# 16-head attentions: values and divisors from one product, divided on VectorE

## The chip, the cores and the metric

The kernel runs on one core of a Trainium2 chip. The metric is the device time of one execution in microseconds; the median of three runs is given with the lowest and the highest. Engines are TensorE (PE, its weight loads PEld), VectorE (DVE), ScalarE (ACT), GpSimd (POOL) and SyncE (SP), which issues most DMAs.

## What is computed

32 sequences of 128 rows and 128 columns go through four layers. Each layer adds to x an attention over a context of 128 rows and 96 columns, and then a feed-forward stage or, in one case, a self-attention with a mixture of experts. All is fp32. Three of the attentions have 16 heads of 8 columns, and they are what the change touches:

```python
x = x + _L0_xattn_ref(_layernorm(x), ctx_768, ...)           # cross: biases, output projection
...
x = x + _L2_xattn_ref(_layernorm(x), ctx_768, mask, ...)     # masked: no projection
x = x + _L2_ffn_ref(_layernorm(x), ...)                      # begins with a causal self-attention, gated
# in each of the three, per head of 8 columns:
attn = softmax(q @ k.T * scale)      # 128 x 128
out = attn @ v                       # 128 x 8
```

The other stages (a one-head and an 8-head attention, experts of four kinds) are not changed but for names.

## The kernel before, in words

The kernel is one program with a phase for each stage. `attention16` builds three of them: cross (`a0_`), masked (`a2_`) and self (`b2_`, `causal`). A phase works on 32 items, one sequence each. It is software-pipelined: `unrolled(last)` yields ticks (called steps here), and in each step every engine runs its stages in an order written out by hand, each stage for another item (`item(lag)`). Each engine takes its instructions in order; between engines there are only semaphores.

The stages of a step that matter here:
- TensorE, cross and masked (L542 on): `pe_turn` (L418, queries and keys turned), `pe_stack_k` and `pe_stack_q` (L424), routing products, `pe_values(e, it, 0)`, turns of the normalised rows, `pe_scoresT` for the first half (L472), `pe_scores` for the first half (L457), `pe_values(e, it, 1)`, the projections (L409, L410), the output product (L514), and the second halves of scores. `pe_stack_q` waits for the maxima of both halves. The self stage has its own order (L519 on).
- `pe_values` (L477 to L493) multiplies the exponentials `P` (keys by queries, one block a head) from the left: with `what == 0` by the item's values in `vx`, with `what == 1` by `ones_x`. In both, four heads of a group are accumulated into the same 32 rows of the bank `OB`; four groups make 128 rows. So `OB[:, 0:128]` holds the values turned (head column by query) and `OB[:, 128:256]` the sums of each head, repeated on its 8 rows. An fp32 product is two instructions in the profile: 32 for the values and 32 for the ones, an item.
- VectorE: `v_max` (L711) takes the row maxima of half an item's scores out of PSUM; `v_heads` (L715 to L724) takes the reciprocal of 128 columns of sums (L719) and multiplies (L723) into `oT`, which the output product reads. In the cross and masked stages the order is keys (L703), statistics, casts, norm, `v_max` first half, `aggregate`, `v_heads`, routing, `v_qkv` (L597 or L600, L610 or L613), residual, `v_max` second half. In the self stage it is `v_max` first half, norm, `v_qk_norm` (L652 on), `v_heads`, routing, `v_max` second half, `v_rotate` (L628 to L641).
- GpSimd in the self stage raises 20 columns to the power -1/2 (L821) between `v_rotate` of one step and `v_qk_norm` of the next.
- `vx` is zero but for the values: head j of a group has its 8 columns at 8j in a block of 32.

Of the kernel before, what the change touches and what calls it, by code (L numbers as in the profile page):

```python
# [18 lines left out]
ALU = mybir.AluOpType  # L19
# [53 lines left out]
def build(nc, a, out):  # L73
    ctx = ExitStack()
    with ctx:
# [134 lines left out]
        ones_x = sb("ones_x", [T, 4, 4, DH])  # L210
# [6 lines left out]
        rec = sb("rec", [D, T])  # L217
# [25 lines left out]
        N_CONSTS = 14  # L243
# [60 lines left out]
        def attention16(p, before, kind, post=None):  # L304
# [26 lines left out]
            s_av, s_rec, s_o = sem("av"), sem("rec"), sem("o")  # L331
            s_out, s_xb, s_done = sem("out"), sem("xb"), sem("done")
# [49 lines left out]
            def pe_post_route(e, item):  # L382
                post["pe_read_by_v"](e)
                if item(O + post["LOGITS"]) or post["last_of"](item(O + post["PLACE"])):
                    e.wait_ge(s_o, at(s_o, issued["av"]))
# [91 lines left out]
            def pe_values(e, it, what):  # L477


                if what == 0:  # L480
                    issued["av"] += 1
                    e.wait_ge(s_exp, at(s_exp, 2 * it.n + 2))
                    e.wait_ge(s_v, at(s_v, it.n + 1))
                    if due(it.n):
                        e.wait_ge(s_o, at(s_o, it.n))
                for j in range(4):
                    for g in range(4):
                        lhs = vx[:, it.s, 128 * j + 32 * g:128 * j + 32 * g + 32] if what == 0 else \
                            ones_x[:, j, :, :].rearrange("p a d -> p (a d)")
                        m = e.matmul(OB[32 * g:32 * g + 32, what * T:(what + 1) * T], lhs,  # L490
                                     P[:, it.s % 2, 4 * g + j, :], start=(j == 0), stop=(j == 3))
                if what == 1:
# [26 lines left out]
            def tensor(e):  # L519
# [6 lines left out]
                if causal:  # L526
                    for item in unrolled(last):
# [6 lines left out]
                        if it := item(L + 3):  # L534
                            pe_values(e, it, 0)
                        if it := item(L + 1):
# [4 lines left out]
                        if it := item(L + 3):  # L541
                            pe_values(e, it, 1)  # L542
# [14 lines left out]
                else:  # L557
                    for item in unrolled(last):
# [7 lines left out]
                        if it := item(L + 3):  # L566
                            pe_values(e, it, 0)
                        if post:
# [7 lines left out]
                        if it := item(L + 3):  # L576
                            pe_values(e, it, 1)
# [137 lines left out]
            def v_heads(e, it):  # L715
                if due(it.n):
                    e.wait_ge(s_o, at(s_o, it.n))
                e.wait_ge(s_av, at(s_av, it.n + 1))
                e.reciprocal(rec[:, :], OB[:, T:2 * T]).then_inc(s_rec, 1)  # L719
                if due(it.n - RING + 1):  # L720
                    e.wait_ge(s_out, at(s_out, it.n - RING + 1))
                e.wait_ge(s_rec, at(s_rec, it.n + 1))
                e.tensor_tensor(oT[:, it.s, :], OB[:, 0:T], rec[:, :], ALU.mult).then_inc(s_o, 1)  # L723
# [2032 lines left out]
```

## Time and profile before

| | before |
|---|---|
| median of 3 runs | 1946.26 us (1944.96 to 1949.05) |
| the profiled execution | 1934.08 us |
| its span, first to last instruction | 1932.3 us |
| PE busy | 1597.6 us, 83% |
| DVE busy | 1342.6 us, 69% |
| ACT busy | 959.0 us, 50% |
| POOL busy | 824.1 us, 43% |
| products with values (L490, `vx`) | 116.5 us |
| products with ones (L490, `ones_x`) | 103.7 us |
| reciprocals of the sums (L719) | 89.8 us |
| granted TensorE clock, mean | 0.916 |

The cross stage fills the span from about 45 to 300 us, the masked one from about 785 to 1060, the self one from about 1070 to 1412. Busy time counts an engine's instructions and not its waits. The granted clock is a share of 2.4 GHz; it has two levels, 1.2 and 2.4 GHz, and a figure between is a mean over a stretch with both.

### The profile page before, as it was taken

How to read it: one execution, taken by the hardware profiler on the slowest of the kernel's cores; microseconds unless marked ns; L12 is line 12 of the kernel's file. 1: busy time of each engine (PE TensorE's matmuls, PEld its weight loads, DVE VectorE, ACT ScalarE, POOL GpSimd, SP SyncE). 2: the span in 40 equal slices, each digit the busy share in tenths (PEclk: the TensorE clock that was granted, in tenths of full speed). 3: DMA queues.
4: the chain of work that ended last, by engine and by line, in shares of the span. 5: the costliest groups of instructions: out<-in, count | busy, mean ns of one | idle time of the engine just before them, and what ended most of it. 6: DMA issues, size and time to landing. Idle time of an engine off the chain costs nothing. (4 is left out here: it accounts for less than half of the span.)

```text
span 1932.3 us, 43308 instructions
## 1 busy us (share of the span) xinstructions
PE 1597.6 (83%) x14686; PEld 1248.9 (65%) x14686; DVE 1342.6 (69%) x4056; ACT 959.0 (50%) x1953; POOL 824.1 (43%) x1300
## 2 busy tenths in 40 slices
PE   5999985977799989788997699999849699999840
PEld 3666664966577778565664466666639598888730
DVE  4878873348787777677775688888647488888522
ACT  2666662533333334366665477777725344444310
POOL 2334444346300000111111777799654555565426
PEclk9989997987799999699999699999969899999965
DMA  6657304821000000000000000000029100000043
GB/s 193 226 181 233 102 12 133 250 71 41 17 1 2 1 1 1 6 8 8 8 7 2 1 2 2 2 9 9 9 80 262 45 15 13 19 20 19 11 147 87
DMA packets 60807, 108.72 MB, mean 56 GB/s; under 512 B 11715, under 2 KB 49620, under 8 KB 59796
## 3 DMA queue, kind: packets, MB, share of 16 engines
q1 hardware_dynamic: 54452, 93.45, 15.6%
q0 software_dynamic: 6144, 12.60, 2.2%
q8 instruction: 116, 1.90, 0.4%
q14 instruction: 95, 0.78, 0.1%
HBM read 89.49 MB, written 52.17 MB: 73 GB/s over the span
## 5 line engine op out<-in xcount | busy, mean ns | idle before, releaser
L711 DVE TENSOR_REDUCE parts<-PS 128x8 fp32r<-128x1024 f32 x192 | 234.5, 1221 | 145.2 <-PE PS L457 145.0
L928 ACT ACTIVATE P<-PS 128x1024 f32<-128x1024 f32 x192 | 198.1, 1032 | 105.4 <-PE PS L472 105.2
L905 ACT CAST qS<-PS 32x512 fp32r<-32x512 f32 x384 | 220.8, 575 | 9.5 <-PE PS L424 6.1
L274 POOL TENSOR_TENSOR ve<-mv,eps_t 128x1 f32<-128x1 f32 x160 | 31.7, 198 | 403.9 <-DVE mv L270 403.5
L1757 DVE SCALAR_TENSOR_TENSOR X<-PS,wt,X 128x128 f32 (+1 forms) x480 | 134.9, 343 | 46.1 <-PE PS L1600 38.3
L1889 ACT ACTIVATE P<-PS,w_f_b 128x512 f32<-128x512 f32 x128 | 88.0, 687 | 142.4 <-PE PS L1581 140.9
L1600 PEld LDWEIGHTS PS<-w_f_w,P 128*128 128x128 f32 x1024 | 129.9, 193 | 39.7 <-issue 27.7
L1600 PE MATMUL PS<-w_f_w,P 128*128 128x128 f32 x1024 | 141.8, 282 | 13.6 <-DVE X L1757 11.8
L472 PE MATMUL PS<-qS,kS 128*128 128x512 f32 x384 | 151.8, 451 | 1.0 <-ACT P L928 1.0
L424 PE MATMUL PS<-ident_r,parts 128*128 128x128 f32 x768 | 124.3, 293 | 27.1 <-issue 26.2
L424 PEld LDWEIGHTS PS<-ident_r,parts 128*128 128x128 f32 x768 | 104.4, 201 | 45.7 <-issue 39.5
L821 POOL TENSOR_TENSOR rrs<-rsq,neg_half 128x20 f32<-128x20 f32 x32 | 114.2, 3569 | 45.0 <-DVE rsq L641 45.0
L490 PE MATMUL PS<-P,vx 128*32 128x128 f32 x3072 | 116.5, 298 | 3.8 <-ACT P L928 3.8
L719 DVE RECIPROCAL rec<-PS 128x128 f32<-128x128 f32 x96 | 89.8, 935 | 26.1 <-PE PS L490 26.0
L490 PE MATMUL PS<-P,ones_x 128*32 128x128 f32 x3072 | 103.7, 276 | 0.0
L457 PE MATMUL PS<-kx,qT 32*128 32x512 f32 x384 | 101.8, 526 | 0.1
L276 POOL TENSOR_TENSOR rstd<-ve,neg_half 128x1 f32<-128x1 f32 x160 | 89.3, 558 | 12.5
L490 PEld LDWEIGHTS PS<-P,vx 128*32 128x32 f32 x3072 | 87.0, 118 | 10.7 <-ACT P L928 4.9
L490 PEld LDWEIGHTS PS<-P,ones_x 128*32 128x32 f32 x3072 | 78.3, 109 | 23.5 <-issue 23.3
L802 POOL TENSOR_TENSOR parts<-qk,parts 128x128 fp32r<-128x128 f32 x192 | 84.9, 462 | 15.9 <-DVE parts L699 13.6
L1413 POOL TENSOR_TENSOR parts<-ident,mx 128x1024 fp32r<-128x1024 f32 x32 | 60.8, 1899 | 52.9 <-DVE mx L1352 52.9
L472 PEld LDWEIGHTS PS<-qS,kS 128*128 128x128 f32 x384 | 69.3, 209 | 20.0 <-issue 15.2
(301 smaller groups left out, 4329.6 us busy)
## 6 DMA issues: line engine op xcount, KB each, us to landing
P<-in_f_blob SPq DMA_DIRECT2D x12, 578.0 KB, 4.8
Y<-in_f_blob SPq DMA_DIRECT2D x11, 578.0 KB, 5.1
ctxT<-in_ctxT SPq DMA_DIRECT2D x128, 48.0 KB, 1.8
tok<-hs SPq DMA_DIRECT2D x46, 128.0 KB, 3.5
hs<-yo SPq DMA_DIRECT2D x46, 128.0 KB, 4.2
P<-in_f_blob SPq DMA_DIRECT2D x12, 450.0 KB, 4.4
Y<-in_f_blob SPq DMA_DIRECT2D x11, 450.0 KB, 4.5
w_f_w<-in_f_w SPq DMA_DIRECT2D x2, 1024.0 KB, 5.7
```

The source lines that it names most:

```text
L276: q.tensor_tensor(rstd[:, it.s, :], ve[:, it.s, :], neg_half[:, 0:1], ALU.pow).then_inc(s_rs, 1)
L424: m = e.matmul(TP[which][:, g * T:(g + 1) * T], parts[:, it.s, which, 4 * g:4 * g + 4, :, :].rearrange("p h c d -> p (h c d)"), ident_r[:, ...
L457: m = e.matmul(S_ps[:, i, :], qT[r:r + 32, it.s, :], kx[r:r + 32, it.s % 2, :, :].rearrange("p j t -> p (j t)"), start=not causal, stop=True)
L472: m = e.matmul(ST_ps[:, i, :], kS[:, it.s % 2, g, :], qS[:, it.s % 2, g, :, :].rearrange("p j t -> p (j t)"), start=not causal, stop=True)
L490: m = e.matmul(OB[32 * g:32 * g + 32, what * T:(what + 1) * T], lhs, P[:, it.s % 2, 4 * g + j, :], start=(j == 0), stop=(j == 3))
L711: e.tensor_reduce(parts[:, it.s, 0, 8 * half:8 * half + 8, 3, 0], S_ps[:, :, :].rearrange("p i (j t) -> p (i j) t", t=T), AXX, ALU.max)\
L719: e.reciprocal(rec[:, :], OB[:, T:2 * T]).then_inc(s_rec, 1)
L821: e.tensor_tensor(rrs[:, :], rsq[:, :], neg_half[:, 0:n_heads], ALU.pow).then_inc(s_rs3, 1)
L905: m = e.copy(qS[r, it.s % 2, :, j, :], TP[0][r, :].rearrange("p (g t) -> p g t", g=4))
L928: e.activation(P[:, it.s % 2, 8 * half:8 * half + 8, :].rearrange("p h t -> p (h t)"), ST_ps[:, :, :].rearrange("p j n -> p (j n)"), ACT.E ...
L1600: m = e.matmul(YP[(n_steps * b + x) % 2][:, s * T:(s + 1) * T], lhs, w2[:, x, t * D:(t + 1) * D], start=(t == 0), stop=(t == tiles - 1))
L1757: m = e.scalar_tensor_tensor(out=X_s, in0=rows, scalar=wt[:, b, s, x:x + 1], in1=X_s, op0=ALU.mult, op1=ALU.add)
```

## The change

The sums come out of the values product itself. Each block of 32 columns in `vx` gets one column of ones among those that its head leaves free: column 16, 17, 0 or 1 for head 0, 1, 2 or 3 of a group. `pe_values` takes a pair of heads instead of values or ones: heads 0 and 1 of all groups go to `OB[:, 0:128]`, heads 2 and 3 to `OB[:, 128:256]`. So of 32 products an item 16 are left, and both pairs are issued where the values product stood; the later place is gone in both orders.

On VectorE the reciprocal and the product out of PSUM are replaced by five instructions. One turns the 256 columns of `OB` by blocks of 32 x 32 into `oV` (queries on partitions), one takes the reciprocal of the 16 sum columns, two multiply the 64 value columns of each pair, and one turns the 128 columns back into `oT`. `OB` is free after the first of them (`values_turned`), and the self and cross stages' routing products wait for that instead of `s_o`. `ones_x` and its memsets go; memsets of the ones columns come in, four on VectorE at the start and four on GpSimd in the one-head stage, behind a memset of `vx`. The 8-head stage uses a view of the new `rec`.

```diff
-        ones_x = sb("ones_x", [T, 4, 4, DH])
+        sum_cols = [vx[:, :, 128 * j:128 * j + 128].rearrange("p r (g c) -> p r g c", c=32)
+                    [:, :, :, (16, 17, 0, 1)[j]:(16, 17, 0, 1)[j] + 1] for j in range(4)]
...
-        rec = sb("rec", [D, T])
+        rec = sb("rec", [T, 2, 4, 2])
+        oV = sb("oV", [T, 2, 4, 32])
+        oN = sb("oN", [T, 4, 32])
+        sums = oV[:].rearrange("p a q r -> p (a q r)")[:, 16:240]\
+            .rearrange("p (a k r) -> p a k r", a=2, k=7)[:, :, 0:7:2, 0:2]
...
-                    e.wait_ge(s_o, at(s_o, issued["av"]))
+                    e.wait_ge(s_tv, at(s_tv, issued["av"]))
...
-            def pe_values(e, it, what):
+            def pe_values(e, it, pair):
-                if what == 0:
+                if pair == 0:
                     issued["av"] += 1
                     e.wait_ge(s_exp, at(s_exp, 2 * it.n + 2))
                     e.wait_ge(s_v, at(s_v, it.n + 1))
                     if due(it.n):
-                        e.wait_ge(s_o, at(s_o, it.n))
-                for j in range(4):
+                        e.wait_ge(s_tv, at(s_tv, it.n))
+                for j in (2 * pair, 2 * pair + 1):
                     for g in range(4):
-                        lhs = vx[:, it.s, 128 * j + 32 * g:128 * j + 32 * g + 32] if what == 0 else \
-                            ones_x[:, j, :, :].rearrange("p a d -> p (a d)")
-                        m = e.matmul(OB[32 * g:32 * g + 32, what * T:(what + 1) * T], lhs,
-                                     P[:, it.s % 2, 4 * g + j, :], start=(j == 0), stop=(j == 3))
-                if what == 1:
+                        m = e.matmul(OB[32 * g:32 * g + 32, pair * T:(pair + 1) * T],
+                                     vx[:, it.s, 128 * j + 32 * g:128 * j + 32 * g + 32],
+                                     P[:, it.s % 2, 4 * g + j, :], start=(j % 2 == 0), stop=(j % 2 == 1))
+                if pair == 1:
                     m.then_inc(s_av, 1)
...
                         if it := item(L + 3):
                             pe_values(e, it, 0)
+                            pe_values(e, it, 1)
...
                         if it := item(L):
                             pe_scores(e, it, 0)
-                        if it := item(L + 3):
-                            pe_values(e, it, 1)
...
             def v_heads(e, it):
+                e.wait_ge(s_av, at(s_av, it.n + 1))
+                if due(2 * it.n):
+                    e.wait_ge(s_on, at(s_on, 2 * it.n))
+                e.transpose(oV[:, :, :, :].rearrange("p a q r -> p (a q r)"), OB[:, 0:2 * T]).then_inc(s_tv, 1)
+                e.wait_ge(s_tv, at(s_tv, it.n + 1))
+                e.reciprocal(rec[:, :, :, :], sums).then_inc(s_rec, 1)
                 if due(it.n):
                     e.wait_ge(s_o, at(s_o, it.n))
-                e.wait_ge(s_av, at(s_av, it.n + 1))
-                e.reciprocal(rec[:, :], OB[:, T:2 * T]).then_inc(s_rec, 1)
+                e.wait_ge(s_rec, at(s_rec, it.n + 1))
+                for pair in range(2):
+                    own_rows = slice(16 * pair, 16 * pair + 16)
+                    e.tensor_tensor(oN[:, :, own_rows].rearrange("p q (h d) -> p q h d", h=2),
+                                    oV[:, pair, :, own_rows].rearrange("p q (h d) -> p q h d", h=2),
+                                    rec[:, pair].unsqueeze(3).broadcast_to([T, 4, 2, DH]), ALU.mult).then_inc(s_on, 1)
                 if due(it.n - RING + 1):
                     e.wait_ge(s_out, at(s_out, it.n - RING + 1))
-                e.wait_ge(s_rec, at(s_rec, it.n + 1))
-                e.tensor_tensor(oT[:, it.s, :], OB[:, 0:T], rec[:, :], ALU.mult).then_inc(s_o, 1)
+                e.wait_ge(s_on, at(s_on, 2 * it.n + 2))
+                e.transpose(oT[:, it.s, :], oN[:, :, :].rearrange("p q r -> p (q r)")).then_inc(s_o, 1)
...
                 e.memset(vx[:], 0.0).then_inc(sem("pad"), 1)
+                e.wait_ge(sem("pad"), at(sem("pad"), 1))
+                for j in range(4):
+                    e.memset(sum_cols[j], 1.0).then_inc(sem("pad"), 1)
```

## Rows read from the trace of the kernel before

**Rows 1.** The page, part 1: busy time, share of the span, instructions.

```profile
PE 1597.6 (83%) x14686; PEld 1248.9 (65%) x14686; DVE 1342.6 (69%) x4056; ACT 959.0 (50%) x1953; POOL 824.1 (43%) x1300
```

**Rows 2.** Groups by line: busy us, mean ns of one, idle before, releaser.

```profile
L490 PE MATMUL PS<-P,vx 128*32 128x128 f32 x3072 | 116.5, 298 | 3.8 <-ACT P L928 3.8
...
L490 PE MATMUL PS<-P,ones_x 128*32 128x128 f32 x3072 | 103.7, 276 | 0.0
...
L719 DVE RECIPROCAL rec<-PS 128x128 f32<-128x128 f32 x96 | 89.8, 935 | 26.1 <-PE PS L490 26.0
```

**Rows 3.** Timeline, one cross step: start us, us taken, what, idle before.

```profile
193.66 1.08 PE L490 MATMUL PS<-P,ones_x 128*32 128x128 f32 x32
...
193.83 1.23 DVE L711 TENSOR_REDUCE parts<-PS 128x8 fp32r<-128x1024 f32 x1 [0.58 <-PE PS L457]
...
195.06 0.93 DVE L719 RECIPROCAL rec<-PS 128x128 f32<-128x128 f32 x1
...
196.09 0.29 DVE L723 TENSOR_TENSOR oT<-PS,rec 128x128 f32<-128x128 f32 x1
...
196.30 0.15 DVE L2230 TENSOR_TENSOR lgD<-PS,w_f_bg 128x8 f32<-128x8 f32 x1
...
197.10 1.22 DVE L711 TENSOR_REDUCE parts<-PS 128x8 fp32r<-128x1024 f32 x1
...
198.41 0.63 PE L424 MATMUL PS<-ident_r,parts 128*128 128x128 f32 x4 [0.38 <-issue]
...
199.35 1.08 PE L490 MATMUL PS<-P,vx 128*32 128x128 f32 x32
...
201.20 0.50 PE L457 MATMUL PS<-kx,qT 32*128 32x512 f32 x2
...
201.81 1.23 DVE L711 TENSOR_REDUCE parts<-PS 128x8 fp32r<-128x1024 f32 x1 [1.35 <-PE PS L457]
```

**Rows 4.** Timeline, one masked step.

```profile
986.29 0.93 DVE L719 RECIPROCAL rec<-PS 128x128 f32<-128x128 f32 x1
...
987.53 0.34 DVE L600 TENSOR_SCALAR qk<-PS,keep 128x128 f32<-128x128 f32 x1
...
993.84 0.92 DVE L719 RECIPROCAL rec<-PS 128x128 f32<-128x128 f32 x1
```

**Rows 5.** Timeline, one self step and the start of the next.

```profile
1232.73 3.54 POOL L821 TENSOR_TENSOR rrs<-rsq,neg_half 128x20 f32<-128x20 f32 x1 [1.76 <-DVE rsq L641]
...
1236.34 0.58 DVE L652 TENSOR_TENSOR ra<-ra,rrs 128x160 f32<-128x160 f32 x1
...
1237.51 0.95 DVE L719 RECIPROCAL rec<-PS 128x128 f32<-128x128 f32 x1
...
1240.07 0.34 DVE L628 TENSOR_TENSOR qkv<-PS,w_b_bqkv 128x192 f32<-128x192 f32 x1
...
1241.65 0.32 DVE L638 TENSOR_TENSOR ra<-ra,rb 128x160 f32<-128x160 f32 x1
...
1242.01 0.32 DVE L639 TENSOR_TENSOR rb<-ra 128x160 f32<-128x160 f32 x1
...
1242.97 3.65 POOL L821 TENSOR_TENSOR rrs<-rsq,neg_half 128x20 f32<-128x20 f32 x1 [1.76 <-DVE rsq L641]
```

**Rows 6.** VectorE groups by line and shape: busy us, mean ns of one.

```profile
L597 DVE TENSOR_TENSOR qk<-PS,w_a_bqk 128x256 f32<-128x256 f32 x32 | 13.3, 416 | 7.2 <-PE PS L410 4.9 <-POOL parts L802 2.2 <-issue 0.2
...
L1358 DVE RECIPROCAL rec<-PS 128x4 f32<-128x4 f32 x64 | 11.5, 179 | 8.0 <-PE PS L1288 6.2
```

**Rows 7.** Windows of a step each: length, busy per engine, granted clock, DMA, GB/s.

```profile
104.10:111.87 7.77, 7.23 (x94) 5.11 (x93) 6.42 (x17) 4.86 (x10) 2.70 (x7) 1.00 0.77 276
...
111.87:121.21 9.34, 8.81 (x94) 6.22 (x94) 6.88 (x21) 5.92 (x11) 2.69 (x7) 0.82 1.04 339
...
1016.47:1025.54 9.07, 8.28 (x90) 5.45 (x90) 5.94 (x15) 5.83 (x10) 1.58 (x4) 0.81 0.01 3
...
1237.51:1247.72 10.21, 9.32 (x102) 6.53 (x102) 9.15 (x30) 7.99 (x19) 7.97 (x14) 1.00 0.01 3
```

More of the change, by code:

```diff
@@ L242, in build @@
         consts_ready = sem("consts_ready")
-        N_CONSTS = 14
+        N_CONSTS = 13
         eps_ready = sem("eps_ready")
@@ L331, in attention16 @@
             s_av, s_rec, s_o = sem("av"), sem("rec"), sem("o")
+            s_tv, s_on = sem("values_turned"), sem("values_normed")
             s_out, s_xb, s_done = sem("out"), sem("xb"), sem("done")
@@ L567, in tensor @@
                             pe_values(e, it, 0)
+                            pe_values(e, it, 1)
                         if post:
@@ L575, in tensor @@
                             pe_scores(e, it, 0)
-                        if it := item(L + 3):
-                            pe_values(e, it, 1)
                         if it := item(F):
@@ L979, in attention16 @@
                    hi=B, lo=2 * B, turn=B, kx=B, qT=B, tk=B, kS=B, tq=B, qS=B, s=2 * B, mx=2 * B,
-                   st=2 * B, exp=2 * B, av=B, rec=B, o=B, out=B, done=B, pad=n_pad)
+                   st=2 * B, exp=2 * B, av=B, rec=B, values_turned=B, values_normed=2 * B, o=B, out=B, done=B,
+                   pad=n_pad)
             if projected and not causal:
@@ L1151, in attention1 @@
             totals(stats=B, rstd=B, h=B, bn=B, ve=B, hps=B, hT=B, qkv=B, qk=2 * B, v=B, s=B, mx=B, nb=B,
-                   exp=B, pps=B, pT=B, av=B, rec=B, done=B, pad=1)
+                   exp=B, pps=B, pT=B, av=B, rec=B, done=B, pad=5)
             totals(**{f"ctx{i}": 16 * GROUPS for i in range(RING)})
@@ L1166, in attention8 @@
             NH, HD = 8, 64
+            rec8 = rec[:, 0].rearrange("p q h -> p (q h)")[:, 0:4]
             s_ctx = [sem(f"ctx{i}") for i in range(RING)]
@@ L1357, in v_heads @@
                     ob = OB[:, :].rearrange("p (h n) -> p h n", n=T)
-                    e.reciprocal(rec[:, 0:4].unsqueeze(2), ob[:, :, HD:HD + 1]).then_inc(s_rec, 1)
+                    e.reciprocal(rec8[:, :].unsqueeze(2), ob[:, :, HD:HD + 1]).then_inc(s_rec, 1)
                     if half == 0:
@@ L1363, in v_heads @@
                     e.tensor_tensor(o8[:, it.s % 2, 256 * half:256 * half + 256].rearrange("p (h n) -> p h n", h=4),
-                                    ob[:, :, 0:HD], rec[:, 0:4].unsqueeze(2).broadcast_to([T, 4, HD]),
+                                    ob[:, :, 0:HD], rec8[:, :].unsqueeze(2).broadcast_to([T, 4, HD]),
                                     ALU.mult).then_inc(s_o, 1)
@@ L2626, in _ @@
             e.memset(vx[:], 0.0).then_inc(consts_ready, 1)
-            e.memset(ones_x[:], 0.0).then_inc(consts_ready, 1)
             e.memset(ones[:], 1.0).then_inc(consts_ready, 1)
-            e.wait_ge(consts_ready, 4)
+            e.wait_ge(consts_ready, 3)
             for j in range(4):
-                e.memset(ones_x[:, j, j, :], 1.0).then_inc(consts_ready, 1)
+                e.memset(sum_cols[j], 1.0).then_inc(consts_ready, 1)
             e.wait_ge(sem("a0_weights"), 16 * n_loads["a0"])
```

## The prediction

> **What bounds the kernel now.** I read the page's part 1 first: TensorE is busy for 83% of the span, VectorE for 69% [rows 1]. That invites the thought that any TensorE work taken out is time won, and the groups by line show how much this change takes out: the products with ones are 3072 instructions that keep the engine busy for 103.7 us, beside 116.5 us for the products with the values [rows 2]. Whether that time is on the path is read from the timeline of single steps in the three 16-head stages, because a share of the span says nothing about order.
>
> In a **cross step** the reader follows VectorE [rows 3]. The first row-maximum (L711) starts at 193.83, when TensorE's first scores are done. From there VectorE runs without a pause: reciprocal 195.06, product with it 196.09, the routing's logits 196.30, then the queries, keys and values out of the bank, the residual, and the second maximum, 197.10 to 198.32. TensorE's second turn (L424) starts at 198.41, as soon as that maximum is there. Then TensorE is the one that runs through: the values product from 199.35, and the next scores from 201.20 to 201.70, and the next first maximum starts at 201.81. So the step is a ring of two pieces: VectorE for 4.5 us, from L711 to the end of L711, and TensorE for 3.4 us. The reciprocal and its product lie in VectorE's piece. The values product lies in TensorE's piece. The **ones product does not**: it runs from 193.66 to 194.74, while VectorE is in its own piece, together with the projections, and nothing that VectorE does next waits for it in a middle step.
>
> A **masked step** has the same order and the same unbroken run of VectorE, from the reciprocal at 986.29 to L600 at 987.53 [rows 4]. A **self step** is another ring, through GpSimd: the power on 20 columns (L821) ends at 1236.27, VectorE takes its result at 1236.34 (L652), does the heads from 1237.51, its second maximum, and the rotation from 1240.07, and hands GpSimd the next sums at 1242.97; GpSimd needs 3.65 us for them [rows 5]. Heads are again in the ring, the ones product is again beside it.
>
> **The change part by part.**
>
> *Products.* 16 products of 32 columns an item in place of 32: the same number of instructions and the same shape as the values product alone has now, so 1.08 us where there were 2.16 [rows 3]. They stand where the values product stood, in TensorE's piece of the ring, and that piece stays as long as it is. What goes is 1.08 us a step beside VectorE's piece: 0 in a middle step. At the ends of a stage it is not hidden, since the ones product then follows the values product at once and the heads wait for it: the waits of the reciprocal on L490 are 26.0 us in the whole run [rows 2]. Most of that is the wait for the first item of a stage, which stays. I take two steps in each stage that get 1.08 us shorter: -6.5 us.
>
> *Heads on VectorE.* Removed: a reciprocal of 128 columns, 0.93 us, and a product of 128, 0.29 us; from the start of the one to the start of what comes next it is 196.30 - 195.06 = 1.24 us [rows 3], 987.53 - 986.29 = 1.24 in the masked stage [rows 4]. Added are five instructions, in a chain. No row shows a transpose on VectorE, nor products of 64 columns, so each is bounded by neighbours:
> - The transpose of 256 columns out of PSUM: 416 ns as L597, which reads as many [rows 6]. Its reader waits for it; between reciprocal and product that costs 196.09 - 195.99 = 0.10 us [rows 3]. 0.52.
> - A reciprocal of 16 columns: 179 ns at 4 columns [rows 6], 935 at 128 [rows 2], so 6.1 ns a column and 0.25 us here. Among operands in SBUF the wait for an own result is smaller, 1242.01 - 1241.65 - 0.32 = 0.04 us [rows 5]. 0.29.
> - Two products of 64 columns. L638 takes 0.32 us for 160 [rows 5]; the slope of plain instructions is 1.05 ns a column (L597's 416 ns for 256 against L711's 1.22 us for 1024) [rows 3, 6], so 0.22 each. The second doesn't wait for the first, and a follower without a wait starts 0.08 us before the end (L2230 at 196.30, L723 ends at 196.38) [rows 3]: 0.14, and 0.26 with the wait behind.
> - The transpose of 128 columns in SBUF: 0.32 - 0.03 = 0.29 by the same row and slope, 0.21 to the start of a follower.
>
> The sum is 0.52 + 0.29 + 0.14 + 0.26 + 0.21 = 1.42 us, 0.18 to 0.19 more than now. **I take +0.19 us a step.** The low end is +0.05, if every wait and each transpose costs less than its neighbour; it isn't under nothing, since L597's row and the reciprocal's slope are floors for two of five. The high end is +0.59: a transpose that takes twice the time a column (256 and 128 more columns at 1.05 ns, 0.40 us). What waits behind: in the cross and masked stages the copies out of the bank, the residual and the second maximum, in front of TensorE's second turn; in the self stage the second maximum and the rotation, in front of GpSimd's power. No idle time of VectorE lies between, so the whole of it is paid: 81 middle steps (32 a stage, less those that fill and empty it) by 0.19 = **+15.4 us**.
>
> A rule of the Trainium skill speaks against this edit: "VectorE: DVE Perf Modes", section "Rules for kernel authors", says that chained operations aren't made cheaper by leaving out semaphores and that the number of operations is what to keep small. Five for two is the wrong way by it, and the trace agrees as far as it goes (0.04 to 0.10 us between dependent instructions). Its section "The three transpose paths" has 311 ns for a 128x128 transpose in bf16; with that in place of 0.29 the edit would cost an estimated +0.21 us a step, 1.6 us more in all.
>
> *The granted clock.* Of the steps in rows 7, one of 7.77 us at full clock is followed by one of 9.34 at 0.82, with the same 94 matmuls: part of it ran at the lower of the two levels, 1.2 in place of 2.4 GHz. Such a fall costs 1.57 us in the cross stage and 9.07 - 7.55 = 1.52 in the masked one, whose undisturbed step is 993.84 - 986.29 = 7.55 us [rows 4, 7]. With a window for each step I count six in the cross stage and seven in the masked one, the last being the third row of rows 7, and none in the self stage. Before each of them TensorE had gone through the thinnest part of its step: behind the ones product, up to the next values product, 199.35 - 194.74 = 4.6 us [rows 3], with narrow products, turns through an identity and waits for VectorE. Without the ones product that part is 7.77 + 0.19 - 1.08 = 6.9 us long. By proportion the 13 falls become 19 or 20. But the new first half of the thin part (projections) is denser than its end and the extra idle time lies at the end, so it can also go to a fall every other step, 28 of the 55 middle steps. I take 25, 12 more: 12 x 1.55 = **+18.6 us**; bounds are 13 fewer (-20: the step's new length may miss the beat that the falls need) and 28 more (+43). In the self stage I take none, for its thin part is filled with the mask's products.
>
> The Trainium skill would have this term at nothing: "TensorE: Matmul & The Clock Gate", section "HAM oscillation — how this bites in real kernels", lets the clock fall where TensorE idles for long between bursts. The rows don't agree: in the step that fell TensorE was busy for 8.81 of 9.34 us.
>
> *The rest.* The bank is free when the transpose has read it, earlier than now; the route's products wait for that in place of the quotient. TensorE isn't waiting for either, so 0. The four memsets more on GpSimd lie at a stage's start behind a memset of 2176 columns, while it waits for DMAs: 0. No DMA is added or moved.
>
> **Sum.** +15.4 + 18.6 - 6.5 = +27.5 us, made against the profiled execution (1934.1 us, of which the span is 1932.3). The median of the three runs is 1946.3, 12 us over it; I put the same difference on it: **1973.8 us**.
>
> **The rivals.**
> 1. *The chain alone.* Falls of the clock stay at 13. For: the self stage shows none although TensorE waits there too, and the extra idle time is only about 1.3 us at a stretch. Against: 13 of 55 middle steps fell with less idle time than that. 1946.3 + 15.4 - 6.5 = 1955.2 us, 1944 to 1965. [...]
> 2. *Slow transposes.* At +0.59 us a step: 81 x 0.59 = 47.8, and 1946.3 + 47.8 + 18.6 - 6.5 = 2006 us. For: nothing in the trace shows one. Against: the other data movers on VectorE all cost about 1.05 ns a column.
> 3. *TensorE was the bound, faster than before.* One mechanism: in cross and masked steps TensorE's side path (ones, projections, second scores) and VectorE's piece are nearly even, so that any shortening of VectorE's piece would have been stopped by the side path, and no longer is. It decides from the point where the new chain takes under 1.24 us, which it does if a transpose hides its fill and its follower starts early. At 1.05 us, and with 6 falls fewer, it gives 1946.3 - 81 x 0.19 - 9 - 6.5 = 1915 us; at a chain of 1.20 and falls as now, 1936. Against: L597's 416 ns alone and the reciprocal's 0.25 leave 0.5 us for three more instructions.
> 4. *It doesn't do what it says.* The reciprocal's gain doesn't come because its fixed part is larger with strided columns: part of 2.
>
> **How the numbers follow.** The forecast 0.50 (its own range 1960 to 1996), rival 1 0.23, rival 2 with 4 0.12, rival 3 0.15. The range takes in rival 1, half of 2 and the upper edge of 3: 1940 to 2004. A difference of 0.2% (3.9 us) is about what a measurement of this kernel can tell from none. Faster by more: rival 3, 0.14. Within it: the lower edge of rival 1 and the rest of 3, 0.11. Slower: 0.75.
>
> **What would show it.** In the profile after: L490 with 3072 matmuls and about 104 to 116 us; the heads from first to last instruction at 1.35 to 1.5 us; the middle masked step without a fall at 7.7, not 7.55; more than 18 steps under a clock of 0.9 in the cross and masked stages; the self step at 10.4, not 10.2. I am wrong if VectorE waits for TensorE ahead of the heads, if the undisturbed steps aren't longer than before, or if the falls are fewer.

## The result and the profile after

| | before | after |
|---|---|---|
| median | 1945.61 us (4 runs, 1944.41 to 1949.05) | 2040.53 us (4 runs, 2036.89 to 2043.48) |
| profiled span | 1932.3 us | 2039.0 us |
| granted TensorE clock, mean | 0.916 | 0.817 |

The kernel after takes 1.0505 times the time of before (95% interval 1.0477 to 1.0533), +94.9 us. The forecast was +27.5 us and a range up to 2004.0: the direction is right, the size is not, and the time lies outside the range. Medians here and below are of all runs, while the ratios leave out slow ones, more than 1.5% above their kernel's fastest: two of six of e5_late, whose ratio so lies below that of the medians, and one of ten of e11_split_fill.

The page of the kernel after, its parts 1 and 2 (the third line is the granted clock in 40 slices of the span, in tenths), answers to rows 1:

```profile
span 2039.0 us, 37548 instructions
PE 1666.4 (82%) x11614; PEld 1287.8 (63%) x11614; DVE 1347.0 (66%) x4343; ACT 964.7 (47%) x1953; POOL 827.0 (41%) x1304
PEclk9857876988799999665556578989987899999965
```

TensorE has 3072 matmuls less and is busy for 69 us more than before. The clock is why: the middle of the masked stage (893 to 1127 us) is the eighteenth to twenty-third digit, 6, 5, 5, 5, 6, 5, and that of the cross stage (82 to 313 us) the second to seventh, 8, 5, 7, 8, 7, 6. The groups by line (answering to rows 2; columns: busy us, mean ns of one | idle us before them, and what ended it) say the same of the products themselves:

```profile
L494 PE MATMUL PS<-P,vx 128*32 128x128 f32 x3072 | 148.3, 354 | 4.4 <-ACT P L941 4.4
L722 DVE STREAM_TRANSPOSE oV<-PS 128x256 f32<-128x256 f32 x96 | 41.1, 428 | 26.9 <-PE PS L494 26.9
```

The values product is as many instructions of the same shape as before, and 148.3 us in place of 116.5.

**The heads** in a cross step of the kernel after, VectorE's timeline (start, us, engine, line), answering to rows 3:

```profile
164.74 0.42 DVE L722 STREAM_TRANSPOSE oV<-PS 128x256 f32<-128x256 f32 x1
165.19 0.25 DVE L724 RECIPROCAL rec<-oV 128x16 f32<-128x16 f32 x1
165.54 0.36 DVE L730 TENSOR_TENSOR oN<-oV,rec 128x64 f32<-128x64 f32 x2
166.01 0.31 DVE L736 STREAM_TRANSPOSE oT<-oN 128x128 f32<-128x128 f32 x1
166.25 0.13 DVE L2248 TENSOR_TENSOR lgD<-PS,w_f_bg 128x8 f32<-128x8 f32 x1
```

From the first to what comes next it is 166.25 - 164.74 = 1.51 us, against 1.24: +0.27 us.

**The middle of each stage** is the best place to compare, since there the pipeline is full. I take 24 steps, from the fifth item's reciprocal to the twenty-ninth's. The windows of the trace (start:end, length, busy time and count of PE, PEld, DVE, ACT and POOL, granted clock, DMA share, GB/s), first of before, then of after, in the order cross, masked, self:

```profile
core 0: us, PE busy (x) PEld busy (x) DVE busy (x) ACT busy (x) POOL busy (x), PEclk, DMA share, GB/s
78.96:278.35 199.39, 185.06 (x2238) 131.28 (x2237) 162.93 (x434) 129.76 (x245) 83.75 (x187) 0.94 0.45 149
848.35:1040.40 192.05, 172.11 (x2111) 115.28 (x2110) 141.77 (x308) 125.29 (x216) 38.08 (x96) 0.94 0.02 7
1146.18:1387.91 241.73, 220.84 (x2409) 153.39 (x2407) 208.85 (x615) 187.39 (x427) 199.82 (x313) 1.00 0.02 6
```

```profile
81.70:313.03 231.33, 200.49 (x1468) 140.73 (x1467) 165.08 (x505) 130.68 (x245) 84.49 (x186) 0.73 0.37 125
893.21:1126.87 233.66, 220.42 (x1341) 142.94 (x1339) 144.44 (x380) 127.86 (x215) 39.70 (x95) 0.57 0.02 5
1240.82:1492.33 251.51, 210.61 (x1642) 145.94 (x1642) 206.46 (x685) 189.02 (x428) 198.73 (x311) 0.93 0.02 5
202.86:210.91 8.05, 6.04 (x62) 4.32 (x60) 6.99 (x23) 5.34 (x10) 3.79 (x9) 1.00 1.11 362
914.00:968.00 54.00, 53.44 (x318) 35.52 (x322) 33.57 (x89) 28.98 (x50) 8.48 (x21) 0.50 0.02 6
```

+31.9, +41.6 and +9.8 us: 83 of the profiled executions' 107 us stand in these 72 steps, and the rest around them. The mean clock fell to 0.73 and 0.57. A mean clock m in a length t stands for t x 2 x (1 - m) us at the lower level (1.2 of 2.4 GHz): 24 and 24 us in the two stages before, 123 and 199 after. The last two rows are the two kinds of step that the kernel after has. At full clock a cross step is 8.05 us (7.77 before, rows 7). At the low level TensorE is busy without a gap, 53.44 of 54.00 us, and is the bound: steps of 9.9 us (masked) and 10.4 (cross), one after the other.

Where TensorE stands idle in a full-clock step of after, its timeline in the cross stage (two rows) and in the self stage (two rows; in brackets the idle time before, and who ended it):

```profile
204.63 0.44 PE L424 MATMUL PS<-ident,qk 128*128 128x128 f32 x2 [1.01 <-DVE vx L613]
206.75 1.08 PE L494 MATMUL PS<-P,vx 128*32 128x128 f32 x32
...
1343.33 0.27 PE L404 MATMUL PS<-ident,h 128*128 128x128 f32 x1
1344.62 0.74 PE L460 MATMUL PS<-causal_q,ident_r 128*128 128x512 f32 x2 [1.02 <-DVE parts L714]
```

The 1.08 us that the ones product leaves empty turn up as one idle piece of 1.0 us: ahead of the turn (L424) in cross and masked steps, and between the two halves of the scores in self ones, where the ones product stood.

### The profile page after: what moved, and what is told of

It reads as the page before. It is cut to its first block and busy times, and to the rows that moved or that the text cites. A ratio compares the mean times of both kernels' runs of the same rounds, so it can differ in the third digit from the quotient of the medians.

```text
span 2039.0 us, 37548 instructions
## 1 busy us (share of the span) xinstructions
PE 1666.4 (82%) x11614; PEld 1287.8 (63%) x11614; DVE 1347.0 (66%) x4343; ACT 964.7 (47%) x1953; POOL 827.0 (41%) x1304
## 3 DMA queue, kind: packets, MB, share of 16 engines
q8 instruction: 92, 1.51, 0.3%
## 5 line engine op out<-in xcount | busy, mean ns | idle before, releaser
L279 POOL TENSOR_TENSOR ve<-mv,eps_t 128x1 f32<-128x1 f32 x160 | 31.9, 199 | 482.6 <-DVE mv L275 482.2
L478 PE MATMUL PS<-qS,kS 128*128 128x512 f32 x384 | 191.8, 562 | 2.9 <-ACT P L941 2.9
L430 PE MATMUL PS<-ident_r,parts 128*128 128x128 f32 x768 | 152.3, 343 | 13.6 <-issue 12.4
L494 PE MATMUL PS<-P,vx 128*32 128x128 f32 x3072 | 148.3, 354 | 4.4 <-ACT P L941 4.4
L430 PEld LDWEIGHTS PS<-ident_r,parts 128*128 128x128 f32 x768 | 133.5, 250 | 28.4 <-issue 22.8
L463 PE MATMUL PS<-kx,qT 32*128 32x512 f32 x384 | 122.7, 636 | 8.7 <-DVE parts L714 8.7
L494 PEld LDWEIGHTS PS<-P,vx 128*32 128x32 f32 x3072 | 107.8, 140 | 16.4 <-ACT P L941 6.1
L478 PEld LDWEIGHTS PS<-qS,kS 128*128 128x128 f32 x384 | 89.6, 269 | 29.8 <-issue 19.9
L463 PEld LDWEIGHTS PS<-kx,qT 32*128 32x128 f32 x384 | 44.6, 229 | 93.4 <-issue 64.4
L460 PE MATMUL PS<-causal_q,ident_r 128*128 128x512 f32 x128 | 49.4, 470 | 35.4 <-DVE parts L714 33.8
L424 PE MATMUL PS<-ident,qk 128*128 128x128 f32 x192 | 50.4, 354 | 33.5 <-DVE vx L613 20.1
```

Source lines behind the costliest of these rows:

```text
L430: m = e.matmul(TP[which][:, g * T:(g + 1) * T], parts[:, it.s, which, 4 * g:4 * g + 4, :, :].rearrange("p h c d -> p (h c d)"), ident_r[:, ...
L463: m = e.matmul(S_ps[:, i, :], qT[r:r + 32, it.s, :], kx[r:r + 32, it.s % 2, :, :].rearrange("p j t -> p (j t)"), start=not causal, stop=True)
L478: m = e.matmul(ST_ps[:, i, :], kS[:, it.s % 2, g, :], qS[:, it.s % 2, g, :, :].rearrange("p j t -> p (j t)"), start=not causal, stop=True)
L494: m = e.matmul(OB[32 * g:32 * g + 32, pair * T:(pair + 1) * T], vx[:, it.s, 128 * j + 32 * g:128 * j + 32 * g + 32], P[:, it.s % 2, 4 * g ...
```

## The experiments

Each ran beside the kernel before, whose median was 1937.9 us in the first group (the first four below), 1941.7 in the second and 1937.8 in the third. "Low" is the time at the lower level in the middle 24 steps, and "falls" how often the clock went down there, both from the clock's record in the trace.

| run | median us | ratio to before | cross: us, low, falls | masked | self |
|---|---|---|---|---|---|
| before | 1945.6 | | 199.4, 24, 7 | 192.1, 24, 7 | 241.7, 0, 0 |
| after | 2040.5 | 1.0505 [1.0477, 1.0533] | 231.3, 123, 11 | 233.7, 199, 7 | 251.5, 38, 9 |
| e1_ones_back | 1981.2 | 1.0234 [1.0197, 1.0272] | 209.1, 34, 9 | 205.8, 41, 11 | 244.8, 0, 0 |
| e2_no_divisors | 2024.0 | 1.0458 [1.0419, 1.0498] | 219.3, 100, 11 | 219.1, 153, 7 | 253.7, 51, 13 |
| e4_split | 2004.6 | 1.0359 [1.0319, 1.0399] | 217.3, 116, 6 | 220.0, 167, 4 | 244.3, 0, 0 |
| e5_late | 1991.0 | 1.0176 [1.0131, 1.0221] | | | |
| e3_filler_early | 2131.6 | 1.0988 [1.0945, 1.1032] | 258.1, 96, 20 | 249.2, 89, 25 | 271.6, 41, 11 |
| e6_fill_turn | 2000.1 | 1.0306 [1.0254, 1.0357] | 194.9, 0, 0 | 187.0, 0, 0 | 288.5, 75, 18 |
| e7_late_fill | 1987.4 | 1.0227 [1.0187, 1.0266] | 204.2, 3, 1 | 194.2, 0, 0 | 267.5, 0, 0 |
| e8_before_fill | 1966.4 | 1.0120 [1.0081, 1.0158] | 193.0, 0, 0 | 181.5, 0, 0 | 268.1, 0, 0 |
| e9_fill_not_self | 1957.8 | 1.0089 [1.0060, 1.0118] | 194.9, 0, 0 | 187.0, 0, 0 | 250.7, 34, 9 |
| e10_before_fill_not_self | 1931.2 | 0.9965 [0.9947, 0.9983] | 191.1, 0, 0 | 181.5, 0, 0 | 242.1, 0, 0 |
| e11_split_fill | 1935.2 | 0.9980 [0.9953, 1.0007] | 198.5, 38, 1 | 184.1, 0, 0 | 244.1, 0, 0 |

**First question: TensorE's side or VectorE's?** One run does each half of the change alone. The first, e1_ones_back, is after with the 16 products with ones put back where they stood, and the heads waiting for them again; VectorE's five instructions stay.

```diff
                         if it := item(L):
                             pe_scores(e, it, 0)
+                        if it := item(L + 3):
+                            pe_filler(e, it)    # 16 products of ones_x with P into OB[:, 256:384], then s_av
```

> The changed kernel with 16 products of ones with P added at the place where before had its ones product (behind the first half of the scores), into 128 free columns of the bank; nothing reads them, and the heads wait for them as they waited before. So TensorE does what it did before and somewhat more (48 instruction pairs less 16: 32 products an item, as before), VectorE does what it does after. Theory A (the product with ones kept TensorE's clock up): the falls go back to about 13, full-clock steps keep the longer chain (0.27 us a step, 81 steps): 1946 + 22 = 1968 us, 1955 to 1985. Theory B (the longer VectorE chain and the waits it brings make the clock fall): it stays over 2010 us, with the granted clock under 0.85.

+43 us (1981.2 - 1937.9), within theory A's range and under half of the change's. The clock is lower than before's, but only by a little, and the self stage keeps it:

```profile
80.68:289.78 209.10, 187.17 (x2238) 133.23 (x2236) 165.25 (x505) 129.93 (x245) 84.62 (x186) 0.92 0.42 141
866.41:1072.24 205.83, 179.56 (x2111) 120.98 (x2109) 145.16 (x380) 125.63 (x215) 39.63 (x95) 0.90 0.02 6
1178.34:1423.15 244.81, 222.30 (x2410) 153.57 (x2408) 211.10 (x686) 187.49 (x427) 201.12 (x313) 1.00 0.02 6
```

81 steps by 0.27 us are at most 22 of the 43. With the longer chain the clock also fell 20 times in the two middles, where before had 14, so VectorE's side has a small part in the low clock too.

The second, e2_no_divisors, is before with the ones product for the first item of each stage alone; VectorE does what it did, and later items are divided by the first one's sums, so the division is not the reference's.

```diff
-                if what == 1:
+                if what == 1 or it.n > 0:
                     m.then_inc(s_av, 1)
...
                             pe_values(e, it, 0)
+                            if it.n == 0:
+                                pe_values(e, it, 1)
...
-                        if it := item(L + 3):
-                            pe_values(e, it, 1)
```

> The kernel before with its product with ones left out for all items but the first of each stage (so the later ones are divided by the first item's sums); its reciprocal of 128 columns and its product on VectorE stay as they were. TensorE does what it does after, VectorE what it did before. Theory A: the clock falls as in the changed kernel, 2041 less the 22 us of the longer chain: 2019 us, 2000 to 2030, and the mean clock near 0.82. Theory B: within 10 us of 1946, a little under it.

Nothing but work (and the heads' wait for it) was taken away, and it costs +86 us; 2024.0 lies in theory A's range. The windows of its cross and masked stretches:

```profile
82.94:302.20 219.26, 191.88 (x1469) 133.24 (x1467) 162.84 (x435) 130.83 (x245) 83.63 (x187) 0.77 0.40 135
882.68:1101.75 219.07, 200.85 (x1341) 131.98 (x1339) 141.87 (x308) 127.00 (x215) 38.04 (x96) 0.65 0.02 6
```

The matmuls of after, VectorE's instructions of before, and 0.77 and 0.65 of the clock. So the missing products bring the low clock without any of the change's instructions on VectorE. The two halves, +86 and +43, are more than the whole, +95: both act through the same clock and cannot be added.

**Second question: does the place of the 16 products matter?** e4_split moves the second pair to the old place of the ones product, e5_late moves both there.

```diff
                             pe_values(e, it, 0)
-                            pe_values(e, it, 1)
...
                             pe_scores(e, it, 0)
+                        if it := item(L + 3):
+                            pe_values(e, it, 1)
```

> The changed kernel with the second pair of products moved to the old place of the ones product; as much work as in the changed kernel, in two lumps of 0.54 us. Theory A1 (what counts is how much TensorE does in a step): falls nearly as many as in the changed kernel, less 0.54 us a step that leave TensorE's piece of the ring in 55 steps (30 us): 2010 us, 1995 to 2025. Theory A2 (what counts is how long the thin part between two lumps is): the thin part is again as long as before, falls as before: 1946 + 22 - 30 = 1938 us, 1925 to 1955.

> The changed kernel with all 16 products moved to the old place of the ones product, behind the first half of the scores. 1.08 us leave TensorE's piece of the ring in the cross and masked steps, and lie beside the first row maximum (1.23 us) instead. Undisturbed cross step 8.05 - 1.08 = about 7.0 us. At full clock 2041 falls out of the sum: 1946 + 22 - 59 = 1909 us. Theory A1: the same work in a shorter step, so fewer falls than in the changed kernel but more than before: 1950 us, 1920 to 1985. Theory A2: the one lump leaves as long a thin part as in the changed kernel less 1 us, so nearly as many falls: 1985 us.

Both are nearer to before, 2004.6 and 1991.0, and still slower. The first fits theory A1 and not A2's 1938. The second lies just over what either theory gave, with runs from 1970 to 2004 us, and doesn't tell the two apart; its profiled execution was the longest of the six, so no stretch of it is given. In the first the clock is as low as after's in cross and masked steps (0.73 and 0.62), yet the self stage has no fall at all, with TensorE no busier there than in after: 202.30 of 244.30 us against 210.61 of 251.51. Its idle time is in smaller pieces. The second row below is the second half of the scores of a self step, 0.45 us behind what came before it instead of 1.02:

```profile
1208.35:1452.65 244.30, 202.30 (x1641) 132.77 (x1640) 211.09 (x686) 187.76 (x427) 201.44 (x313) 1.00 0.02 5
...
1340.01 0.73 PE L460 MATMUL PS<-causal_q,ident_r 128*128 128x512 f32 x2 [0.45 <-DVE parts L716]
```

**Third question: the amount of TensorE's work, or the idle piece?** Two runs add the same number of products, 16 of 32 columns, to the kernel after. e3_filler_early puts them right behind the values, so that the idle piece stays. e6_fill_turn puts them into it; they multiply constants and write into `TP[0]`, which the next stack overwrites.

```diff
                             pe_values(e, it, 0)
                             pe_values(e, it, 1)
+                            pe_filler(e, it)            # the first run
...
+                        if it := item(L + 1):
+                            pe_fill_turn(e, it, range(4))   # the second: ident by ident into TP[0]
                         if it := item(L):
                             pe_turn(e, it)
```

> The kernel after, with 16 more products of 32 columns (the old ones products, into a part of OB that nobody reads) right behind the values in all three 16-head stages; the 16 come before the heads may start, so they lie on the ring: 1.0 us a step at full clock, 81 steps = +81 us if nothing else changed. Theory A' (the clock stays down because TensorE has 16 products less to do in a step, wherever they stand): the clock returns to mean 0.90 or more, each middle stretch of 24 steps of the cross stage has under 50 us at 0.5, and the time is about 1981 (the run with the ones product at its old place) plus 0 to 81: 1980 to 2060. Rival (what counts is where the products stand, the gap ahead of the turn): the clock stays at 0.82 and the time is 2040 plus 81 to 160, over 2100.

> The kernel after, with 16 products of 32 columns of a constant (into TP[0], which the next stack overwrites) at the top of a step, ahead of the turn, where TensorE stood idle for 1.0 us of an undisturbed cross step. They cost nothing at full clock as long as the idle time holds them. Theory A' (amount): the clock comes back to mean 0.90 or more and the time falls to about 1960 to 1985, near the run with the ones product back (1981) or below it. Rival (the missing work doesn't matter, or only work with real data in its old place): the time stays at 2020 to 2060 at a mean clock of 0.82.

This tells them apart. The first has 32 products a step as before, and its clock falls once in nearly every step: 20 and 25 times in 24 steps. A masked step of it, and its turn's row:

```profile
1000.02:1010.30 10.28, 8.29 (x88) 6.02 (x88) 6.05 (x17) 5.21 (x9) 1.66 (x4) 0.83 0.02 6
...
1002.29 0.44 PE L425 MATMUL PS<-ident,qk 128*128 128x128 f32 x2 [1.06 <-DVE vx L625]
```

The second has no fall in the cross and masked stretches:

```profile
78.71:273.56 194.85, 171.67 (x2236) 122.83 (x2235) 165.19 (x505) 129.80 (x245) 84.97 (x186) 1.00 0.45 150
849.41:1036.38 186.97, 160.91 (x2109) 108.12 (x2107) 144.45 (x380) 124.99 (x216) 39.97 (x95) 1.00 0.03 7
1155.41:1443.91 288.50, 251.30 (x2411) 174.47 (x2410) 196.88 (x685) 190.34 (x428) 196.89 (x309) 0.87 0.02 5
...
936.26 1.08 PE L503 MATMUL PS<-ident 128*32 128x128 f32 x32
937.27 0.44 PE L424 MATMUL PS<-ident,qk 128*128 128x128 f32 x2
```

The filler runs from 936.26 and the turn starts at 937.27 with no idle time before it. 36.5 and 46.7 us came back in the two stretches. I had expected the amount to decide and a mean clock of 0.90 or more in the first; it was 0.866, at 2132 us. My theory fell there: with the same number of products, the piece left idle ahead of the turn goes with 45 falls, the filled one with none. The filled piece also makes TensorE's idle time less, in the masked stretch 249.2 - 200.2 = 49 us in the first and 187.0 - 160.9 = 26 in the second, so these two runs don't tell the one piece from the sum of idle time; the self stages of after (nine falls) and e4_split (none) do, with nearly the same sum, 41 and 42 us.

That the length of the longest idle piece alone decides is not shown, and the trace of before speaks against it. TensorE's waits in its masked stretch, which has seven falls, are no longer than those in the stretch of e6_fill_turn, which has none (us in total, times, longest; two rows of before, then two of e6_fill_turn, which has a single wait of 1.0 us besides):

```profile
PE PS L424 <- issue: 12.1, 24, 0.5
PE PS L418 <- DVE vx L613: 7.9, 24, 0.6
...
PE PS L415 <- ACT hT L943: 14.1, 23, 0.6
PE PS L430 <- issue: 10.7, 24, 0.5
```

One of the two stands ahead of the stack in both (L424, L430). The other stands ahead of the turn in before (L418) and ahead of the projections in e6_fill_turn (L415). Why the place counts is open.

The self stage lost 37 us with the filler, since there the turn doesn't stand behind idle time and the filler is on the path; that is why the time, 2000.1, lies between both forecasts. So the next run, e9_fill_not_self, leaves the self stage as it is in after.

> The kernel after with the 16 constant products ahead of the turn in the cross and masked stages alone; the self stage is that of the kernel after. With the filler in all three stages the middle 24 steps took 194.9 us (cross) and 187.0 (masked) with no fall, and 288.5 (self). Here 195, 187 and 251.5 against 199.4, 192.1 and 241.7 before: 0 us to before within 10, about 1940 to 1955, of which the self stage is +10. If it comes out so, nearly all of the change's +95 in cross and masked was the clock, and the chain of 0.27 us a step is what is left where there are no falls. If it stays over 1980, something other than the stages' steps carried the loss.

1957.8 us, 1.0089 times before, a little over the forecast's 1955. Adding 1984 matmul instructions whose result nobody reads takes the ratio from 1.0505 to 1.0089, which is 0.0416 x 1945.6 = 81 us. The mean clock was 0.815 to 0.827 in the four runs of after and 0.892 to 0.910 in the six of this one, so it is not the traced execution alone. Its cross stretch is the same as in the run above, at full clock; below it the filler's group of the whole run:

```profile
84.42:279.28 194.86, 171.78 (x2236) 122.78 (x2235) 165.15 (x505) 129.74 (x245) 84.79 (x186) 1.00 0.45 150
...
L503 PE MATMUL PS<-ident 128*32 128x128 f32 x1984 | 71.2, 287 | 0.0
```

**Fourth question: is there something better than both kernels?** e7_late_fill is the late order with 8 products ahead of the turn and 8 ahead of the transposition of `h`. e8_before_fill is before with 8 products ahead of the turn, e10_before_fill_not_self the same without the self stage. e11_split_fill is the split order with 8 over all column groups, without the self stage. (A column group is one of the four bands of 32 rows of the output that the products write.)

```diff
+                        if it := item(L + 1):
+                            pe_fill_turn(e, it, range(2))   # 8 products, two of the four column groups
                         if it := item(L):
                             pe_turn(e, it)
```

> All 16 products at the old place of the ones products (1991 without filler), with 8 constant products ahead of the turn and 8 in the wait ahead of the transposition of h. If the amount of work holds the clock up and the filler lies in idle time: undisturbed steps of 7.3 to 7.7 us in cross and masked, mean clock 0.90 or more, and 1915 to 1950, at or below the kernel before (1942). If the filler does not hold the clock: 1990 or more. If it holds the clock but is on the ring, 1950 to 1985.

> The kernel before, with 8 constant products at the top of a step ahead of the turn. If more work on TensorE keeps the clock up further, its 14 falls in the two middle stretches of cross and masked (about 1.5 us each) go, which is worth up to -22 us, against a cost of up to 0.5 us a step where there is no idle time (81 steps: +43): 1920 to 1985. Theory A' expects fewer us at 0.5 in cross and masked than before (23.9 and 23.9); a rise would speak against it.

> The kernel before with the 8 constant products ahead of the turn in cross and masked alone. From the run with them in all three stages: 193.0 and 181.5 us in the middle stretches against 199.4 and 192.1, and the self stage as before, 241.7. Sum -17 us, so 1920 to 1930 against 1942: faster than both kernels. If the falls that vanish were worth nothing (the steps only get longer by the filler), 1942 to 1960.

> The run with the second half of the products at the old place of the ones product (2004.6), with 8 constant products over all four column groups (0.54 us) ahead of the turn in cross and masked, where TensorE stood idle for 0.43 to 0.65 us. If the idle time ahead of the turn is what lets the clock fall: steps of 7.6 us, 183 us for the middle stretches of both stages, self 244: 1915 to 1935. If the sum of TensorE's work is what counts (24 products of the after's kind in a step, against 32 before), falls remain and the time is 1950 to 2000.

With the late products the clock is held and the fillers lie on the path: 1987.4, just over the 1985 put down for that case. In all three stages the filler costs before's self stage 26 us (268.1 for 241.7), and the time is 1966.4, but the cross and masked middles have no fall; in the run without the self stage both stretches are the shortest of all runs:

```profile
81.40:272.49 191.09, 190.06 (x2622) 140.91 (x2621) 164.33 (x435) 129.29 (x245) 83.44 (x187) 1.00 0.47 156
849.26:1030.77 181.51, 180.94 (x2495) 127.47 (x2494) 141.83 (x308) 124.92 (x216) 38.09 (x96) 1.00 0.03 8
```

They are 8.3 and 10.5 us shorter than before's, of which only 6.6 us arrive in the time: 1931.2 us against 1937.8, where I had expected 17 and at most 1930 us. In its profiled execution the parts outside the three stages' middles are 15.5 us longer than in before's (1314.6 for 1299.1), with 309 us at the lower level there for 277; with single executions of each I can't say that this is more than their spread. It is the only version clearly faster than before, by 0.35%. The split order with the filler is the fastest form of the change, 0.998, not to be told from before. Its middle masked stretch is 184.1 us without a fall; the cross one has a single fall that lasts 38 us, in a profiled execution of 1956 us, where the ten runs take 1927 to 1962. So 8 products don't always hold the clock there; how often they do, one trace cannot show.

## Why the prediction was wrong

- **The bound, and the ones product's place.** Right. Nothing in the middle steps waited for the ones product, and its removal shortened none: at full clock the median cross and masked steps of e2_no_divisors are 7.78 and 7.54 us, of before 7.80 and 7.54.
- **Heads on VectorE, +0.19 us.** The right mechanism, 0.08 short: +0.27, and an undisturbed cross step is 8.05 us against 7.77. Item by item, to the start of the next: transpose of 256 columns 0.45 (I took 0.52), reciprocal 0.35 (0.29), two products 0.47 (0.40), transpose of 128 columns 0.24 (0.21). The two waits inside SBUF cost 0.10 and 0.11 us, not the 0.04 of rows 5, and the one behind the transpose out of PSUM 0.03, not 0.10. By 81 steps that is +22 for +15.4, as an upper end: with fillers in both, the middles of cross and masked differ by (194.9 - 191.1) + (187.0 - 181.5) = 9.3 us in 48 steps, 0.19 a step (the filler of before may cost a little itself, since its idle time is shorter), and the self stage of e1_ones_back is 244.8 - 241.7 = 3.1 us longer in 24 steps, 0.13 a step.
- **The transposes.** 0.42 and 0.31 us; the slope from neighbours gave 0.42 and 0.29. The Trainium skill, "VectorE: DVE Perf Modes", section "The three transpose paths", has 311 ns for the second in bf16; this trace has the same 311 ns for fp32. Rival 2 is out.
- **The clock, +18.6 us.** This is the step that failed. I took 12 more steps with a fall (13 to 25) at 1.55 us each, the price of rows 7, where a fall is over within its step. Counted the same way (steps under a clock of 0.9), the 48 middle cross and masked steps have 14 before and 43 after. By the runs at full clock the low clock cost after 36.5 + 46.7 = 83 us in these two stretches, and before 8.3 + 10.5 = 19: net +64 in the middles alone, for +18.6. That is 29 more steps at 2.2 us each, so both factors were too low, the count most of all. The falls themselves are hardly more, 18 for 14: what I had wrong is how long a fall lasts. Before, the 14 made 48 us at the low level. After, the 18 made 123 + 199 = 322 us, 18 us each on average and 75 us the longest. The bound of 28 more falls (+43) follows from nothing in the text either: a fall every other step is 28 in all, 15 more.
- **No falls in the self stage.** Wrong: nine. I said its thin part was filled with the mask's products. What I did not look for was the place where the ones product had been the only work: between the two halves of the scores, where 1.02 us stand idle once it is gone. With half of the products there the falls went (0 in 244.3 us).
- **Drains, -6.5 us.** Didn't come: VectorE's waits for the products are 26.9 us against 26.0 [rows 2]. Whether the shorter drains were hidden or lost to the clock wasn't tried apart.
- **The sum.** Between the two profiled executions: clock +64 and chain +9.3 in the 48 middle cross and masked steps, +9.8 in the 24 of the self stage, of which 3.1 chain; that is 83 of 107 us. Of the other 24, 10 stand between the middles of cross and masked and 8 between those of masked and self, and the clock is lower there too, 0.86 for 0.90 and 0.69 for 0.85 (two windows of before, then the same two of after):

```profile
278.35:848.35 570.00, 473.85 (x3429) 396.55 (x3428) 375.61 (x1453) 228.91 (x493) 140.40 (x203) 0.90 0.15 45
1040.40:1146.18 105.78, 78.25 (x758) 49.71 (x758) 69.23 (x208) 58.89 (x118) 62.05 (x98) 0.85 0.00 1
...
313.03:893.21 580.18, 485.57 (x3175) 403.56 (x3173) 376.78 (x1477) 229.59 (x493) 140.78 (x209) 0.86 0.14 44
1126.87:1240.82 113.95, 82.24 (x501) 51.51 (x500) 69.13 (x230) 58.89 (x117) 63.10 (x100) 0.69 0.00 1
```
- **The rivals.** None had it. Rival 1 kept the falls at 13, rival 3 went the other way, and rival 2 came nearest (2006 us) by a slow transpose that isn't there.

Rows 7 gave me a price for a fall that comes back within its step, and I carried it over to a kernel in which TensorE has other work. No row of before shows a whole step of these stages at the low level, so the case "it stays down" needed a bound of its own, and had none. With the trace of after it can be given: a step takes 9.9 us (masked) there for 7.55, so all 55 middle cross and masked steps at the low level are about 55 x 2.4 = +130 us. A bound of that size would have kept the measured time inside the range.

**Open.** Why the low clock lasts so long in after, with TensorE busy throughout (53.44 of 54.00 us). The number of products in a step goes with it: in the cross and masked middles the longest stretch at the low level that begins there is 3.4 us in before and 6.8 in e1_ones_back and e3_filler_early, all with 32 products a step, and 75, 58 and 51 us in after, e2_no_divisors and e4_split, with 16. e3_filler_early leaves the same idle piece open as after and has 45 falls and 184 us low, after 18 and 322. So filling the idle piece ahead of the turn stops the falls, and the work in a step goes with how soon the clock returns. How either comes about I have not shown.

## What to carry to other kernels

Before taking work out of an engine that waits, find where the hole will be and how long it is in one piece: on TensorE, a hole of 1.0 us in a step of 8 was worth 83 us over 48 steps, and filling it with products of no use gave that back. Price a fall of the clock by how long it stays down, not by how often it comes, and keep the case "it stays down" in the range. If work must go, move what is left into the hole: half of it there took 2040.5 us to 2004.6, all of it to 1991.0.

## What the chip showed that I had not expected

- Less work on TensorE, with all other engines' work as before, made the kernel 1.0458 times as long (e2_no_divisors).
- TensorE's clock stayed at 1.2 GHz for 54 us at a stretch while it was busy for 53.44 of them. The Trainium skill, "TensorE: Matmul & The Clock Gate", section "HAM oscillation — how this bites in real kernels", ties falls to long idle time between bursts. The direction agrees with the filler runs, but here pieces of 1.0 us were enough; that the clock stays down under full work is not in that section and is what cost most here.
- Eight products of 32 columns over two of the four column groups take as long as sixteen over four: 1.07 us, as the row of e8_before_fill shows, and 1.08 us, L503 above:

```profile
933.58 1.07 PE L498 MATMUL PS<-ident 128*32 128x128 f32 x16
```
